# An attention and mixture-of-experts layer: every expert's branch written out, and one-tile units computed by rows and turned

## The reference

```python
x = L0_attn_x                                   # (4, 1024, 256), float32
xn = _layernorm(x)
q, k, v = xn @ Wq.T + bq, xn @ Wk.T + bk, xn @ Wv.T + bv
qk = q @ k.T                                    # per batch, 1024 x 1024
theta = 0.5 + 0.2 * sigmoid(qk) + 0.15 * tanh(qk) + 0.1 * relu(qk)
s = (softmax(theta) @ v) @ Wo.T + bo
e = argmax(softmax(xn @ Wr + br))               # one of 8 experts per token
y = gelu(xn @ W1[e] + b1[e]) @ W2[e] + b2[e]    # 256 -> 1024 -> 256, exact gelu
out = x + s * silu(y)
```

## Time and profile before

| | us |
|---|---|
| median of 3 runs | 550.07 |
| lowest, highest | 549.77, 550.94 |
| the profiled execution | 549.93 |
| its span, first to last instruction | 548.1 |
| TensorE busy | 526.6 (96%) |
| VectorE busy | 413.5 (75%) |
| ScalarE busy | 337.6 (62%) |
| GpSimd busy | 206.3 (38%) |

### The profile page before, as it was taken

How to read it: one execution, slowest core, us unless ns; L and a number is a source line. 1 busy time by engine, 2 the same in 40 slices (tenths; PEclk the granted TensorE clock), 3 DMA queues, 4 the chain that set the end, 5 groups by cost and what they waited for, 6 DMA issues and landing times.

```text
span 548.1 us, 11163 instructions
## 1 busy us (share of the span) xinstructions
PE 526.6 (96%) x3891; PEld 496.4 (91%) x3892; DVE 413.5 (75%) x808; ACT 337.6 (62%) x607; POOL 206.3 (38%) x246
## 2 busy tenths in 40 slices
PE   7999999999999999999999989799999999999996
PEld 6888898998999999999999979798899899999995
DVE  6896688945588754787554897768899999777895
ACT  3587778536356733466433666278777877777881
POOL 2216338923112222122122214304467585333442
PEclk9999999999999999999999999999999999999999
DMA  8932920044315711146211411004132232111121
GB/s 285 333 153 107 337 78 1 1 139 160 125 59 150 245 45 50 46 148 226 85 38 52 130 50 39 19 21 155 59 108 95 88 115 88 59 42 46 59 67 49
DMA packets 40306, 56.88 MB, mean 104 GB/s; under 512 B 3607, under 2 KB 35358, under 8 KB 39726
## 3 DMA queue, kind: packets, MB, share of 16 engines
q1 hardware_dynamic: 35020, 45.62, 24.8%
q0 software_dynamic: 3488, 9.47, 6.0%
q10 hardware_dynamic: 1762, 1.32, 0.7%
HBM read 40.68 MB, written 17.56 MB: 106 GB/s over the span
## 4 chain that ended last, share of the span: by engine, by line
PE 79%; DVE 10%; ACT 5%; issue 4%; DMA 1%; DVEq 0%; ACTq 0%
PE ps L813 25%; PE ps L815 23%; PE ps L814 23%; PE ps L912 4%; PE ps L972 2%; PE ps L1085 1%; DVE stats L1220 1%; DVE theta L1278 1%; DVE theta L1274 1%; PE ps L962 1%; ACT theta L613 1%; ACT theta L603 1%; DMA xn_all<-in_L_attn_x_dram 1%; ACT tanh_s L604 1%; DVE u_lo L1255 0%
## 5 line engine op out<-in xcount | busy, mean ns | idle before, releaser
L712 ACT ACTIVATE hid<-ps,b_now 128x256 f32<-128x256 f32 x160 | 66.7, 471 | 42.3 <-PE ps L815 32.7
L813 PE MATMUL ps<-v_hi,pT_hi 128*128 128x258 f32 x256 | 76.2, 298 | 2.5 <-DVE pT_lo L1292 1.0
L814 PE MATMUL ps<-v_lo,pT_hi 128*128 128x258 f32 x256 | 72.5, 283 | 0.0
L815 PE MATMUL ps<-v_hi,pT_lo 128*128 128x258 f32 x256 | 72.3, 282 | 0.0
L1274 DVE SCALAR_TENSOR_TENSOR theta<-tanh_s,theta 128x512 f32<-128x512 f32 x64 | 49.1, 767 | 27.5 <-ACT tanh_s L604 26.8
L813 PE MATMUL ps<-rowT_h,w_hi_even 128*128 128x256 f32 x224 | 63.8, 285 | 1.1 <-issue 1.0
L815 PE MATMUL ps<-rowT_h,w_lo_even 128*128 128x256 f32 x224 | 63.5, 283 | 0.0
L814 PE MATMUL ps<-rowT_l,w_hi_even 128*128 128x256 f32 x224 | 63.4, 283 | 0.0
L483 POOL COPY unit_token<-sorted_token 128x2 int32 x19 | 4.6, 241 | 152.3 <-PE ps L1085 152.3
L613 ACT ACTIVATE theta<-theta,neg_max 128x512 f32<-128x512 f32 x64 | 42.9, 721 | 28.2 <-DVE neg_max L1278 27.9
L813 PE MATMUL ps<-w_hi_even,hidT_h 128*128 128x256 f32 x200 | 58.1, 291 | 0.2
(11 more groups left out here) (228 smaller groups left out, 1664.0 us busy)
## 6 DMA issues: line engine op xcount, KB each, us to landing
w_raw_odd<-in_L_ffn_W_dram SPq DMA_DIRECT2D x10, 1024.0 KB, 5.3
w_raw_even<-in_L_ffn_W_dram SPq DMA_DIRECT2D x6, 1024.0 KB, 6.6
sorted_g<-g_sb SPq DMA_DIRECT2D x20, 256.0 KB, 2.1
xn_rows<-xn_all SPq DMA_DIRECT2D x4, 1024.0 KB, 6.0
x_tile<-in_L_attn_x_dram SPq DMA_DIRECT2D x32, 128.0 KB, 2.2
out_dram<-g_tile SPq DMA_DIRECT2D x32, 128.0 KB, 1.7
xn_all<-in_L_attn_x_dram SPq DMA_DIRECT2D x3, 1024.0 KB, 12.1
kept_xT<-passing_xT SPq DMA_DIRECT2D x2, 1024.0 KB, 4.3
```

The lines of the kernel that those rows point to most:

```text
L712: last = nc.scalar.activation(hid[:, j % 2, c * UNIT:(c + 1) * UNIT], ps[:, HID_BANK + j, c * UNIT:(c + 1) * UNIT], ACT.Gelu, bias=b1_now[ ...
L813: mm(dst, a_hi, b_hi, start=first, stop=False)
L814: mm(dst, a_hi, b_lo, start=False, stop=False)
L815: return mm(dst, a_lo, b_hi, start=False, stop=last)
```

## The change

1. All experts are written out on TensorE, VectorE and ScalarE; the loop over pairs is gone. Within an expert, full units run in a loop and a one-tile unit in code of its own behind it. TensorE loads all limits ahead of time, between products of tiles 5 and 6; the other two load the next expert's limits in the current one, and ScalarE picks the next expert's bias (`pick_b1`) there.
2. A one-tile unit is computed by rows: the tile's rows are the stationary operand, and 512 columns of weights the moving one (`half_rows`, 12 matmuls). Its 128 x 1024 result is copied to memory (half by ScalarE, half by VectorE), turned by eight transposes (`half_turned`), and gelu, high and low parts follow in steps of 2, 2 and 4 blocks.
3. The inner weights are split by their output columns and no longer by their input rows, and `hidden` waits for the second half at its middle only. VectorE makes the first half of the next outer weights in the expert's first unit.
4. Batch 2's parts move from GpSimd to ScalarE and VectorE, in expert 7's first unit. Tile 8's activations move from there to the unit before the last.
5. Around the last unit: `job(9)` goes between products and turns of the last unit, and tile 8's values go ahead of tile 9's transposes.
6. In the first part: ScalarE's second copies of the turned batch 3 go ahead of tile 1's activations, and its square root ahead of `transposed_high(0)`. On VectorE, `scales(3)` goes ahead of `transposed_parts(0)`, `take_turned` ahead of `low_v(0, 3)` and `finish(0)`, and `finish(2)` ahead of the slots' calculation.

```diff
             def low_w1(e):
-                for i, piece in enumerate(halves(w1_hi[0])):
+                for i, cols in enumerate(HIDDEN_HALVES):
...
-            pool.wait_ge(kept_in, 16)
-            wait_apart(pool, y_done, before_last)
...
-                    last = nc.gpsimd.tensor_copy(xnT_hi[place_of_batch(2)][:, k, cols], own_xT[:, k, cols])
...
             exps(0)
-            acts(1, 0)
             for q in range(2, 4):
                 keep_turned(0, q)
-            acts(1, 1)
-            transposed_high(0)
+            for h in range(2):
+                acts(1, h)
...
+            def gelus_half(u, par):
+
+                act.wait_ge(hid_done, u * 4 + 1)
+                act.wait_ge(hidT_ready, u * 4 + 1)
+                nc.scalar.activation(hid[:, 0, :], ps[:, HID_BANK, :], ACT.Copy).then_inc(gelu_done, 1)
+                for s in range(1, 4):
+                    first, stop = HALF_STEPS[s]
+                    act.wait_ge(hid_done, u * 4 + 3 + stop // 8)
+                    for c in range(first, stop):
+                        last = nc.scalar.activation(
+                            half_gelus(s)[:, c - first, :], ps[:, HID_BANK + 2 + c // 4, c % 4 * P:(c % 4 + 1) * P],
+                            ACT.Gelu, bias=b1_now[:, par, c:c + 1])
                     last.then_inc(gelu_done, 1)
...
+            with act.If(u7 < last_u):
+                gelus(u7, 1)
+                row_high(u7 + 1)
+                wait_apart(act, y_done, u7)
+                high_xT(2)
+                gate(u7)
...
+            def half_rows(u, par, split):
+
+                pe.wait_ge(rowT_ready, u + 1)
+                for h in range(2):
+                    if h:
+                        pe.wait_ge(w1_split, split)
+                    for k in range(DC):
+                        last = product(ps[:, HID_BANK + h, :], rowT_h[:, k, 0:P], rowT_l[:, k, 0:P],
+                                       w1_hi[par][:, k, HIDDEN_HALVES[h]], w1_lo[par][:, k, HIDDEN_HALVES[h]],
+                                       k == 0, k == DC - 1)
+                    last.then_inc(hid_done, 1)
...
+            def units(e):
+
+                par, split, u0, full, u1 = e % 2, (e + 1) * 2, end_of[e - 1] if e else 0, full_of[e], end_of[e]
+                pe.wait_ge(w1_split, split - 1)
+                with pe.If(u0 < full):
+                    with nc.Fori(u0, full, engines=bass.OrderedEngineSet([mybir.EngineType.PE]),
+                                 head_slot={mybir.EngineType.PE: par * 128}) as u:
+                        hidden(u, par, split)
+                        turn_rows(u + 1)
+                        pe.wait_ge(w2_split, split)
+                        expert_out(u, par)
+                with pe.If(full < u1):
+                    half_rows(full, par, split)
+                    half_turned(full, following=True)
+                    pe.wait_ge(w2_split, split)
+                    half_out(full, par)
...
+            job(TPB + 1)
+            with pe.If(last_u < full_7):
+                wait_apart(pe, gelu_done, last_u * 4 + 2)
+            with pe.If(full_7 < end_7):
+                half_turned(last_u)
+            scores(TPB + 1)
...
                 if n == TPB + 1:
-                    job(n)
...
+                    wait_apart(pe, y_biased, end_of[E - 1])
+                    weighted(n - 1)
+                    transposes(n)
...
             thetas(1)
+            scales(3, TPB, 3 * TPB)
             transposed_parts(0)
-            scales(3, TPB, 3 * TPB)
...
             thetas(4)
             transposed_parts(3)
+            finish(2)
             dve.wait_ge(ranks_done, 1)
...
+            def parts_half(u):
+
+                dve.wait_ge(hid_done, u * 4 + 2)
+                v.tensor_copy(hid[:, 1, :], ps[:, HID_BANK + 1, :]).then_inc(hidT_ready, 1)
...
+                for i, cols in enumerate(HIDDEN_HALVES):
+                    dve.wait_ge(w1_high, e * 2 + i + 3)
+                    v.tensor_tensor(w1_lo[other][:, :, cols], raw[:, :, cols],
+                                    w1_hi[other][:, :, cols].bitcast(F32), ALU.subtract).then_inc(w1_split, 1)
+                low_w2(e, other, 0)
+                following = limits_of(e + 1)
+                dve.wait_ge(b2_in, e * 16 + 16)
                 biased(u, par)
```

404 lines of the change are left out of this document (228 added, 176 removed).

## The result

| | before | changed |
|---|---|---|
| median of 4 runs each, us | 549.92 | 537.8 |
| lowest, highest | 549.42, 550.94 | 537.60, 537.91 |
| profiled execution, its span | 549.93, 548.1 | 537.6, 535.9 |
| ratio, 95% interval | | 0.9777 [0.976, 0.9794] |

A forecast was written before the change was run, and what follows sets the result against it. TensorE, busy 96% of 548.1 us, was taken to bound the kernel. Eight gains summing to 15.7 us, off 549.93, gave 534.2 us; own range 531.5 to 536.5, wide range (8 in 10) 529.5 to 541.

The forecast's parts named there:

- The chain of a one-tile unit: Last units of experts 0 and 2: engines' hand-overs followed step by step give 8.35 us, 1.3 gained each, 2.6 together.
- Experts 1 and 3: Their ends: limit loads leave TensorE's stream, a branch comes in; 0.3 us gained for both, between -0.8 and 0.7.
- Experts 5 and 6: Narrower VectorE parts and weights split by output columns let expert 7 begin earlier; 2.7 us gained, between 0.5 and 4.
- First unit of expert 7: Idle time in small pieces, clock stays, but VectorE arrives late; 0.8 us gained, between -0.8 and 1.6.
- Second unit: Expert 7: batch 2's parts leave GpSimd, tile 8's scores move to the unit behind; 4.0 us gained, between 3.0 and 4.0.
- Last unit and return: Last unit to attention's return: cheaper products, attention product fills the chain's gap; 18.4 us, 2.7 gained, between 1 and 3.5.
- Ahead of the experts: First part: reordered ScalarE and VectorE work shortens four TensorE waits; 2.1 us gained, between 0.5 and 3.2.
- Rival 1: Short one-tile units do not pay: gaps cost 1.3 more each or the clock falls; 5 to 6 lost, 540 us; 17%.
- Rival 2: Early orders only move waits and VectorE is still late at expert 7; 2.1 and 1.5 lost, 537.5 us; 13%.
- Rival 3: TensorE's seven forward jumps over expert bodies cost 3.1 us each, 21.7 in all; 556 us, slower; 5%.
- Rival 4: One-tile chain better hidden than counted, and early waits go whole; 4 more gained, 530 us; 10%.
- Rival 5: No unit takes the short path, so the change does not do what it says; 6.8 lost, 541 us; 1%.

The follow-up runs named there:

- by_columns: Changed kernel with its four one-tile units sent through the old 48 products of 256 columns, all else left; 542.09 us.
- last_limits_early: Changed kernel with the two register loads of the last units' numbers moved one expert forward on ScalarE and VectorE; 537.44 us.
- limits_spread: Changed kernel with TensorE's 16 limit loads spread singly over batch 1's query and value products; 536.29 us against 537.68 for the changed kernel.
- limits_twice: Changed kernel with each of the 16 limit loads between the products of tiles 5 and 6 done twice; 553.59 us.

## Why the prediction held, and where not

The total came out 3.6 above the forecast, outside its own range of 531.5 to 536.5 and inside the wide one, which had taken in the rivals. The parts were off by more: those that gained less than forecast fell short by 5.1 in all, and those that gained more made up 1.6 of it.

*The chain of a one-tile unit.* Right in its steps, 8.54 measured for 8.35: 1.1 gained in each of experts 0 and 2 instead of 1.3. What my working did not say is that half of this is no gain of rows: `by_columns` makes the same unit in 9.07. The old one's 0.66 at its end was a matter of loads and loop, and goes with either form.

*Experts 1 and 3*: 0.85 measured (11.95 for 12.40 and 12.35), 0.3 forecast. The branch over the one-tile body costs nothing that can be seen, and 0.4 at each end went.

*Experts 5 and 6*: 1.8 measured, 2.7 forecast; mis-sized in my chain for expert 6, which took 10.73 for 9.4. The copy of the first half waited for ScalarE's four loads and branches (1.02, of which `last_limits_early` gives back 0.54), where I had put such loads on VectorE alone. Rows brought 0.3 of the 1.8; the other 1.5 is there in `by_columns` too (22.99 for both experts), and belongs to the weights' split, VectorE's order and the loads; of these only two of the loads were moved by themselves (0.57).

*First unit of expert 7*: 1.5 measured, 0.8 forecast. VectorE was not late. *Second unit*: 4.0, as forecast; putting the parts back costs 3.1 of it, and the hold-up of before was 0.9 longer (6.18 for 5.26).

*Last unit and return*: 2.2 up to tile 11's scores, 2.7 forecast, and then 1.1 more lost at the next turns, which I had at nothing. I followed the chain to tile 9's turns and stopped one tile too early: VectorE still had tile 9's parts behind tile 10's thetas there.

*Ahead of the experts*: the step that failed. Forecast 2.1, measured -0.2, and only the entry of expert 0 did better (0.9 for 0.5). The waits of the earlier trace rows went as I had said, and the early orders gained 2.5 up to tile 6. But I wrote that the limits' loads "now stand in the attention part, between products" and gave them no price there. They cost 1.64. And part of the early gain would not have arrived without them either: `limits_spread` is 2.4 ahead of the kernel before at tile 6 (94.13 for 96.55) and 0.9 at the gathered rows (121.37 for 122.29). Of that loss 0.6 is the wait for `token_at`, at which the kernel before arrives too late to meet it, and 0.45 is loads.

*The rivals.* Rival 1: no; the gaps cost what was counted, and the clock stayed 1.00 (314 to 321 has four gaps of 0.4 to 1.0). Rival 2 named the right total (537.5) by luck: the gain ahead of the experts did not arrive, but 1.6 of it went to the loads and only 0.6 would have gone to a wait that moved, and VectorE was not late at expert 7. Rival 3: from 125.73 to 298.54 TensorE's only waits are four for `hidT_l` in the two short units, 1.9 together, so none of the jumps in experts 1, 3 and 4 cost anything. The branch instructions themselves are not all short. In the changed kernel most take TensorE's sequencer 0.07 to 0.4, but the one at the head of expert 4's loop takes 0.85 and the jump over expert 6's full unit 1.02, both with matmuls still running, so that nothing is lost. At the head of expert 7's loop, behind the wait for `w_lo_odd`, no matmuls are left to cover one, and its 0.40 stands open (0.37 to 0.78 in the other kernels). So a jump costs 1.0 at most in this execution and not 3.1, and mostly under cover. By the rule of the Trainium skill (Runtime: NRT & Kernel Launch, Instruction fetch mechanics) a branch out of the pages held stalls. The trace has long branches, but how much code TensorE holds, and whether these jumps leave it, no run here tells. Rival 4: no, the chain was hidden no better than counted. Rival 5: no, the matmul counts are those of the short path.

*Slips in the working.* The losses of rival 2, 2.1 and 1.5, make 537.8 and not 537.5. The chain of the last unit adds up to 18.2, not 18.4, and in "2.74 of products (5.76 less 3.02)" the two numbers have changed places: 3.02 is saved and 2.74 left. The clock of the last stretch before was 0.99. None of this moves the forecast by more than 0.3.

What stays open: in `limits_twice` TensorE stands still for 2.22 at the entry of expert 0. Its sequencer is held by one branch, at the head of the expert's loop (L1209), which takes 3.54 there and 0.32 in every other profiled run of the changed kernel's form. That is a stall of the kind and size that rival 3 named, once in one execution. What made it is not shown: the DMA engines are fully busy at that time, but they are as busy at the same place of the changed kernel.
